# A rewritten preparation, two chunks interleaved ahead of attention, and operands loaded by halves in a fused macaron-block kernel

## The chip, the cores and the metric

The kernel runs on one core of one Trainium2 chip, as one launch. The metric is device time in microseconds (us) of that core; a kernel's time is the median of its runs.

## The reference

```
x = x + 0.5 * ffn(layernorm(x))            # pass A, x is (4, 1024, 128)
x = x + attn(layernorm(x))                 # 16 heads of 8, rotary, ALiBi, softmax over all 1024 keys
x = x + 0.5 * ffn(layernorm(x))            # pass C

def ffn(x):
    shared = relu2(x @ up_w.T) @ down_w.T                 # 512 hidden columns
    scores = sigmoid(x @ gate.T)                          # 8 experts, best group of 2, top 2, normalised
    lat    = x @ fc1_w.T
    routed = sum_e coef_e * (relu2(lat @ w1[e].T) @ w2[e].T)
    return shared + routed @ fc2_w.T

def attn(x):
    q, k, v = heads(x @ qkv_w.T); q, k = rotary(q), rotary(k)
    s = q @ k.T * 8**-0.5 + 8 * slope_h * min(key - query, 0)
    return (softmax(s) @ v) @ proj_w.T + proj_b
```

## The kernel before

The 4096 tokens are 8 chunks of 512 (two halves of each of 4 batches). The program has a preparation block (lines 200 to 370), then one fused block of five engine streams (from line 521), then two blocks that run only when a bound on the scores fails; in the profiled execution only the test of that bound is made.

The preparation loads all weights, turns them on TensorE, folds fc1 with w1 and w2 with fc2, and splits them in a high and a low part (`w_hi`, `w_lo`), since most products are made of three passes (`times_weights`, L709). VectorE collects the weights in `w_all`, ScalarE copies the high part, VectorE subtracts. All its loads are issued by SyncE, the first two x chunks, the rotary table and the row of positions last. The fused block begins when every engine has left the preparation.

In the fused block each chunk is a job of pass A (`("A", c)`: layer norm, router, FFN, residual, second norm, rotary q and k, v) and, after its attention, a job of pass C (`("C", c)`: projection, norm, router, FFN, residual, store). Attention runs over 256 "quads": 32 groups (chunk, four heads) of 8 key tiles. A quad is four score matmuls of 512 columns into the four banks `scores` (L729), one ScalarE exponential of 128x2048 (`weight`, L977), on half of the quads a VectorE multiplication by `ediag` (L1334), and four matmuls with v into `acc` (`weigh`, L748). The four score banks are a single set, so the next quad's scores wait for the exponential.

The order is written out: `PLAN` gives each job's operations a step, every engine walks over the same steps and does at each step what the plan and `+1` rules say (`rectify = hidden + 1`, and so on), and waits for semaphores. Quad n is at step `HEAD_STEPS + n`. Before the first quad (`HEAD_STEPS` = 58) stand jobs A0 and A1, nearly all of A2 (32 of 40 matmul operations) and a third of A3 (13 of 40); after the last quad (from step 314) stand 10 operations of C5, 31 of the 32 of C6 and all of C7. An engine's stream is strictly in order. In a job the relu of a hidden tile is ScalarE's (L945), the square or the product of relu and expert coefficient is GpSimd's (L1003) behind VectorE's `scale` (L1231), the router is VectorE's (`route1` to `route5`, L1142 to L1216), `res` the end of the FFN (L1237). `relu` is a ring of four tiles that every job shares, as are `xn`, `xn_t` and the banks `bank_h`, `bank_c`, `bank_o`; only in the "wide" jobs A0, A1 and C7 are the score banks used as second banks.

The rotary q and k are split in parts and stored to DRAM (L640), and loaded again, transposed by address, as the operands `q_op`, `k_full`, `k_plain`: per batch 4 groups x 12 loads of both halves at once (`load_parts`, L2076) and 8 loads of the shift row (L675). All are SyncE's. The rows of these operands that don't come from DRAM are filled by GpSimd at the first 12 steps (`fill_rows`). The load of the x chunk of A3 (L634) follows the residual of A1 in the plan. `ediag` is made in the preparation.

## Time and profile before

| what | us |
|---|---|
| median of 3 runs | 897.0 (896.61 to 901.86) |
| profiled execution, its own time | 895.53 |
| span of that execution, first to last instruction | 893.7 |
| preparation, to the first instruction of the fused block | 22.35 |
| first exponential of attention | 163.5 |
| end of the last exponential | 824.1 |
| last residual | 874.8 to 875.5 |

The page gives for the span of 893.7 us: TensorE busy 755.8 us (85%), VectorE 468.2 (52%), ScalarE 577.5 (65%), GpSimd 239.1 (27%). Times in the rows are microseconds from the start of the span unless they say ns. The 1.8 us between the span and the execution's own time lie outside the instructions.

### The profile page before, as it was taken

How to read it: one execution, taken by the hardware profiler on the slowest of the kernel's cores; microseconds unless marked ns; L12 is line 12 of the kernel's file. 1: busy time of each engine (PE TensorE's matmuls, PEld its weight loads, DVE VectorE, ACT ScalarE, POOL GpSimd, SP SyncE). 2: the span in 40 equal slices, each digit the busy share in tenths (PEclk: the TensorE clock that was granted, in tenths of full speed). 3: DMA queues.
4: the chain of work that ended last, by engine and by line, in shares of the span. 5: the costliest groups of instructions: out<-in, count | busy, mean ns of one | idle time of the engine just before them, and what ended most of it. 6: DMA issues, size and time to landing. Idle time of an engine off the chain costs nothing. (4 is left out here: it accounts for less than half of the span.)

```text
span 893.7 us, 14584 instructions
## 1 busy us (share of the span) xinstructions
PE 755.8 (85%) x5517; PEld 372.6 (42%) x5517; DVE 468.2 (52%) x1171; ACT 577.5 (65%) x439; POOL 239.1 (27%) x207
## 2 busy tenths in 40 slices
PE   3567781889899999989999899989999999989881
PEld 2456560334344334434434344334444344434561
DVE  4877771744634755462563553653554635354770
ACT  2121110578778877777887788977888788888220
POOL 1855440401301331221231122221122211213350
PEclk9997996799999999899999999999999999999996
DMA  6002057111122451120233210034421001010100
GB/s 217 1 23 71 25 136 171 38 39 28 40 77 68 100 149 51 28 64 19 70 87 99 66 47 4 16 91 100 104 62 53 5 5 54 4 52 4 55 12 20
DMA packets 42071, 52.64 MB, mean 59 GB/s; under 512 B 9528, under 2 KB 27392, under 8 KB 41856
## 3 DMA queue, kind: packets, MB, share of 16 engines
q1 hardware_dynamic: 41984, 51.53, 21.7%
q8 instruction: 49, 0.80, 0.4%
q14 instruction: 38, 0.31, 0.1%
HBM read 31.85 MB, written 19.40 MB: 57 GB/s over the span
## 5 line engine op out<-in xcount | busy, mean ns | idle before, releaser
L977 ACT ACTIVATE weights<-f_scores 128x2048 f32<-128x2048 f32 x256 | 481.0, 1879 | 126.8 <-PE f_scores L729 121.4
L748 PE MATMUL f_acc<-weights,v_res 128*9 128x512 f32 x2048 | 270.1, 599 | 12.7 <-DVE weights L1334 11.5
L1334 DVE TENSOR_TENSOR weights<-weights,ediag 128x512 f32<-128x512 f32 x128 | 92.8, 726 | 113.2 <-ACT weights L977 112.9
L824 PE MATMUL f_bank_o<-w_out,f_hid 128*128 128x128 f32 x1024 | 146.2, 288 | 2.3 <-POOL f_hid L1003 1.8
L1003 POOL TENSOR_TENSOR f_hid<-f_hid,f_relu 128x512 f32<-128x512 f32 x64 | 86.6, 1357 | 228.1 <-DVE f_hid L1231 226.8
L824 PEld LDWEIGHTS f_bank_o<-w_out,f_hid 128*128 128x128 f32 x1024 | 125.6, 194 | 51.9 <-issue 40.0
L1003 POOL TENSOR_TENSOR f_hid<-f_relu 128x512 f32<-128x512 f32 x64 | 68.0, 1068 | 251.9 <-ACT f_relu L945 248.5
L945 ACT ACTIVATE f_relu<-f_bank_h 128x512 f32<-128x512 f32 x116 | 69.0, 595 | 83.3 <-PE f_bank_h L709 80.8
L729 PE MATMUL f_scores<-q_op,k_plain 29*128 29x512 f32 (+3 forms) x768 | 86.8, 441 | 19.8 <-ACT weights L977 15.8
L729 PEld LDWEIGHTS f_scores<-q_op,k_plain 29*128 29x128 f32 x768 | 37.5, 183 | 137.0 <-ACT weights L977 112.8
L709 PE MATMUL f_bank_h<-f_xn_t,w_hi 128*128 128x512 f32 x232 | 86.4, 454 | 9.5 <-ACT f_relu L945 6.8
L1231 DVE TENSOR_TENSOR f_hid<-f_relu,f_bank_c 128x512 f32<-128x512 f32 x58 | 39.7, 685 | 95.7 <-ACT f_relu L945 88.1
L729 PE MATMUL f_scores<-q_op,k_full 29*128 29x512 f32 (+3 forms) x640 | 62.1, 375 | 7.6 <-ACT weights L977 5.6
L748 PEld LDWEIGHTS f_acc<-weights,v_res 128*9 128x9 f32 x2048 | 31.3, 88 | 72.6 <-issue 60.2
L709 PEld LDWEIGHTS f_bank_h<-f_xn_t,w_hi 128*128 128x128 f32 x232 | 36.5, 195 | 57.8 <-issue 41.9
L729 PEld LDWEIGHTS f_scores<-q_op,k_full 29*128 29x128 f32 x640 | 31.6, 185 | 51.2 <-ACT weights L977 50.2
L709 PE MATMUL f_bank_h<-f_xn_t,w_lo 128*128 128x512 f32 x116 | 47.2, 407 | 0.0
L810 PE MATMUL f_bank_c<-f_coef_t,spread_rows 128*128 128x512 f32 x58 | 24.8, 427 | 25.9 <-DVE f_hid L1231 25.8
L1327 DVE COPY f_o_out<-f_acc 128x512 f32<-128x512 f32 x32 | 22.0, 688 | 28.1 <-PE f_acc L748 28.1
L1019 POOL TENSOR_TENSOR f_squares<-f_roped 128x512 bf16<-128x512 f32 x16 | 19.5, 1218 | 56.6 <-DVE f_roped L1272 49.9
L991 POOL TENSOR_TENSOR f_rstd<-f_veps,f_minus_half 128x4 f32<-128x4 f32 x24 | 24.3, 1011 | 36.8 <-DVE f_veps L1096 36.8
L709 PEld LDWEIGHTS f_bank_h<-f_xn_t,w_lo 128*128 128x128 f32 x116 | 22.6, 195 | 5.6
(165 smaller groups left out, 703.6 us busy)
## 6 DMA issues: line engine op xcount, KB each, us to landing
q_parts<-f_parts SPq DMA_DIRECT2D x24, 256.0 KB, 3.0
k_parts<-f_parts SPq DMA_DIRECT2D x24, 256.0 KB, 3.0
q_op<-q_parts SPq DMA_DIRECT2D x64, 96.0 KB
k_full<-k_parts SPq DMA_DIRECT2D x64, 96.0 KB
k_plain<-k_parts SPq DMA_DIRECT2D x64, 96.0 KB
o_scratch<-f_o_out SPq DMA_DIRECT2D x128, 18.0 KB
x_ln<-in_L_attn_x_dram SPq DMA_DIRECT2D x8, 256.0 KB, 2.9
rope<-const_rope SPq DMA_DIRECT2D x1, 2048.0 KB, 9.5
```

Of the source, the lines that this page charges most:

```text
L709: last = nc.tensor.matmul(out, w[:, col:col + P], x_t[:, part, :], start=(i == 0), stop=(i == 2))
L729: last = nc.tensor.matmul(scores[:, j, lo:hi], k_op[rows, g, kt * P:(kt + 1) * P], q_op[rows, g, CHUNK * half + lo:CHUNK * half + hi], sta ...
L748: last = nc.tensor.matmul(acc[BLOCK * j:BLOCK * j + VW, :], v_res[:, c // HALVES, kt, col:col + VW], weights[:, n % 2, j, :], start=(kt == ...
L810: nc.tensor.matmul(spread_bank(job, m), spread_rows[:, m * P:(m + 1) * P], coef_t[:, :], start=True, stop=True).then_inc(spread, 1)
L824: last = nc.tensor.matmul(bank_o[:, t * P:(t + 1) * P], hid[:, m, t * P:(t + 1) * P], w_out[:, m, :], start=(m == 0 and t == 0), stop=(m = ...
L945: nc.scalar.activation(relu[:, at % RELUS, :], hidden_bank(job, m), ACT.Relu).then_inc(relu_ready, 1)
L977: nc.scalar.activation(weights[:, n % 2, :, :], scores[:, :, :], ACT.Exp).then_inc(exps_done, 1)
L991: nc.gpsimd.tensor_tensor(rstd[:, which, :], veps[:, which, :], minus_half[:, :], ALU.pow).then_inc(rstd_ready[which], 1)
L1003: nc.gpsimd.tensor_tensor(hid[:, m, :], other, relu[:, at % RELUS, :], ALU.mult).then_inc(hid_ready, 1)
L1231: v.tensor_tensor(hid[:, ST + m, :], relu[:, at % RELUS, :], spread_bank(job, m), ALU.mult).then_inc(scaled_ready, 1)
L1327: v.tensor_copy(o_out[:, :], acc[:, :]).then_inc(acc_read, 1)
L1334: v.tensor_tensor(at, at, ediag[:, GH * g:GH * (g + 1), :], ALU.mult).then_inc(diag_done, 1)
```

## The change

1. Preparation. The weight loads are split over two issuing engines: SyncE issues the fold weights, the two x chunks, the tables, `diag` and `rope`; ScalarE issues up, qkv, gate, the slopes, down, proj, a new constant `turn` and the positions. `w_all` is gone: ScalarE writes the high parts straight from the banks and VectorE subtracts from the banks. The rotated columns come from a matmul with `turn`. The norm of chunk 0, up to both parts of its turned tile, is made here too, its square root on GpSimd. `sdiag` is gone; GpSimd's memset of `v_res` covers only the columns of ones, and GpSimd fills `k_plain` of two groups.
2. Jobs A0 and A1 (`HEAD_JOBS`). They are interleaved over 222 finer steps, each operation with a step of its own (`own=...`, kept in `job.at`). A1 has its own banks (`acc` for `bank_o`, `scores[:, 1]` and `[:, 3]` for the gate and the turn) and tiles (`twin_xn`, `twin_xn_t`), and relu tiles of both are not in the shared ring. In these two jobs the squares are ScalarE's and only once per tile (`relu` squared, then VectorE multiplies by the coefficient), and ScalarE also copies the coefficients and the high parts of q and k.
3. ScalarE also fills `q_op` and `k_full` (`FILLS`, 8 instructions of 128x1024) and makes `ediag` (`DIAGONALS`, 16 exponentials of 128x128 with a scale) during these steps.
4. Operands of batch 0. They are loaded per half and group: 8 times 12 loads of 48 KB, and per group 2 loads of the shift row. Group 0's first half follows the store of A0; the rest follows the shift, or the quads. Group 0's shift rows are issued by ScalarE. Scores wait for `first_loaded`, `late_plain` and `late_loaded`.
5. The plan. The first quad is at step 222 with A0 and A1 complete and 12 of the 40 matmul operations of A2 ahead of it; 9 instead of 3 of the 256 attention steps are without an operation of a job. After the last quad (from step 478) stand 14 operations of C4, 31 of C5 and all 32 of both C6 and C7. The x load of A3 is at step 130.

```diff
-HEAD_STEPS = 58
+HEAD_JOBS = 2
+HEAD_STEPS = 222
+FILLS = (2, 69, 151, 118, 6, 109, 51, 59)
+DIAGONALS = (136, 133, 156, 137, 141, 142, 144, 123, 132, 125, 146, 122, 139, 147, 131, 128)
 PLAN = (
+    ("A", 0, dict(front=(0, 0, 0), norm=(-9, -9, -9, 0), route=(8, 13, 18, 23, 28), coef=35,
+        hidden=(3, 7, 12, 21, 25, 30, 41, 49), spread=(39, 48, 55, 62),
+        outs=(15, 15, 27, 27, 32, 32, 44, 44, 52, 52, 56, 56, 64, 64, 70, 70), residual=77,
+        norm2=(80, 93, 124), qk=(140, 143, 150, 157), value=(152, 152), norms=(168, 183),
...
+    ("A", 1, dict(front=(0, 0, 0), norm=(1, 16, 19, 37), route=(43, 53, 60, 67, 72), coef=90,
+        hidden=(61, 68, 73, 78, 83, 91, 99, 107), spread=(98, 106, 114, 119),
+        outs=(75, 75, 86, 86, 94, 94, 102, 102, 111, 111, 115, 115, 120, 120, 126, 126), residual=130,
+        norm2=(138, 158, 163), qk=(174, 176, 179, 182), value=(187, 187), norms=(191, 199),
...
+            def square(job, m):
+
+                act.wait_ge(relu_ready, HT * job.index + m + 1)
+                tile = relu_tile(job, m)
+                nc.scalar.activation(tile, tile, ACT.Square).then_inc(squared, 1)
...
+            def fill_rows(i):
+
+                which, g = divmod(i, HG)
+                op, factor, add = ((q_op, row_sel[:, 6:7], q_add1), (k_full, row_sel[:, 3:4], k_add1))[which]
+                nc.scalar.activation(op[:, g, :], pos, ACT.Identity, bias=add[:, g:g + 1], scale=factor).then_inc(rows_filled, 1)
...
+            def first_operands(step):
+                if step == FIRST_JOB[0].at["store"][1] + 1:
+                    load_half(0, 0, first_loaded[0], first_loaded[0])
+                if step == FIRST_JOB[1].at["fill"] + 1:
+                    sp.wait_ge(shift_ready, 1)
+                    load_half(1, 0, late_plain, late_loaded)
+                    load_half(0, 1, first_loaded[1], first_loaded[1])
+                    load_shift_rows(sp, 0, 1, first_loaded[1])
+                for g in range(1, HG):
+                    if g >= 2 and step == HEAD_STEPS + KT * (g - 1) + 2:
+                        sp.wait_ge(shift_ready, 1)
+                        load_half(0, g, first_loaded[g], first_loaded[g])
+                        load_shift_rows(sp, 0, g, first_loaded[g])
+                    if step == HEAD_STEPS + KT * (g - 1) + 4:
+                        sp.wait_ge(late_plain, 16 * GH * g)
+                        sp.wait_ge(late_loaded, 16 * (PART_LOADS - GH) * g)
+                        load_half(1, g, late_plain, late_loaded)
...
+                if half == 0 and batch == 0 and kt == 0:
+                    pe.wait_ge(first_loaded[g], 16 * (PART_LOADS + HALVES))
+                elif half == 0 and batch == 0 and kt == TILES:
+                    pe.wait_ge(late_plain, 16 * GH * (g + 1))
+                elif half == 1 and batch == 0 and kt == 0:
+                    pe.wait_ge(late_loaded, 16 * (PART_LOADS - GH) * (g + 1))
```

## Rows read from the trace of the kernel before

**Rows 1.** Windows: us, busy (instructions) per engine, granted TensorE clock, DMA share, GB/s.
```profile
core 0: us, PE busy (x) PEld busy (x) DVE busy (x) ACT busy (x) POOL busy (x), PEclk, DMA share, GB/s
0.00:22.35 22.35, 8.20 (x28) 5.62 (x28) 9.61 (x27) 6.17 (x7) 4.13 (x6) 1.00 0.64 217
22.35:60.28 37.93, 23.63 (x121) 19.74 (x122) 28.07 (x72) 6.42 (x12) 25.83 (x24) 0.96 0.00 1
60.28:96.11 35.83, 28.49 (x142) 22.68 (x141) 27.31 (x77) 7.41 (x13) 17.68 (x15) 0.81 0.20 59
96.11:122.20 26.09, 17.39 (x84) 11.13 (x83) 22.30 (x61) 6.09 (x11) 15.31 (x14) 1.00 0.21 61
122.20:137.00 14.80, 12.03 (x78) 9.33 (x78) 11.56 (x41) 2.98 (x5) 5.11 (x5) 1.00 0.69 165
137.00:157.90 20.90, 0.49 (x5) 0.25 (x3) 0.00 (x0) 1.08 (x2) 0.00 (x0) 0.61 0.75 163
...
163.50:824.10 660.60, 618.78 (x4784) 268.73 (x4784) 328.69 (x795) 534.46 (x367) 145.05 (x123) 0.99 0.21 55
824.10:876.00 51.90, 43.03 (x273) 33.05 (x269) 35.10 (x86) 12.25 (x22) 22.48 (x20) 1.00 0.10 29
876.00:893.70 17.70, 0.00 (x0) 0.00 (x0) 0.00 (x0) 0.00 (x0) 0.00 (x0) 0.58 0.09 25
```

**Rows 2.** Waits between 124 and 163 us.
```profile
DVE f_stats L1077 <- DMA x_ln<-in_L_attn_x_dram: 21.3, 1, 21.3
```

**Rows 3.** Timeline of SyncE's issues: start, us, instruction.
```profile
125.01 0.33 SPq L2076 DMA_DIRECT2D q_op<-q_parts  x1
...
145.39 4.46 SPq L675 DMA_DIRECT2D q_op<-f_shift  x8
...
150.39 0.50 SPq L634 DMA_DIRECT2D x_ln<-in_L_attn_x_dram  x1
```

**Rows 4.** Timeline of ScalarE, first quads; its idle time before in brackets.
```profile
163.55 1.88 ACT L977 ACTIVATE weights<-f_scores 128x2048 f32<-128x2048 f32 x1 [1.42 <-PE f_scores L729]
166.33 1.88 ACT L977 ACTIVATE weights<-f_scores 128x2048 f32<-128x2048 f32 x1 [0.91 <-PE f_scores L729]
169.83 1.88 ACT L977 ACTIVATE weights<-f_scores 128x2048 f32<-128x2048 f32 x1 [1.62 <-PE f_scores L729]
172.32 1.88 ACT L977 ACTIVATE weights<-f_scores 128x2048 f32<-128x2048 f32 x1 [0.61 <-PE f_scores L729]
```

**Rows 5.** Timeline: second weight set turned, `sdiag`, last split, first gate.
```profile
8.88 0.48 PE L306 MATMUL prep<-ident,raw_up 128*128 128x128 f32 x1 [2.33 <-DMA raw_proj<-in_L_attn_proj_w_dram]
...
15.64 2.28 DVE L349 TENSOR_TENSOR sdiag<-diag,slope 128x2048 f32<-128x2048 f32 x1
...
21.39 0.68 DVE L369 TENSOR_TENSOR w_lo<-w_all,w_hi 128x512 fp32r<-128x512 f32 x1
...
33.66 0.21 PE L775 MATMUL f_bank_c<-w_gate,f_xn_t 128*128 128x16 f32 x1
```

**Rows 6.** Timeline of VectorE: a norm's centring, a router's first and 16th instruction, statistics.
```profile
67.90 1.10 DVE L1100 TENSOR_SCALAR f_xn<-f_res,f_mean,f_rstd 128x128 f32<-128x128 f32 x4
...
87.59 0.19 DVE L1142 TENSOR_TENSOR f_en<-f_en 128x32 f32<-128x32 f32 x1 [2.66 <-ACT f_en L937]
...
92.21 0.42 DVE L1195 TENSOR_REDUCE f_rank<-f_above 128x32 f32<-128x256 f32 x1
...
98.82 0.86 DVE L1077 BATCH_NORM_STATS2 f_stats<-f_res 128x6 f32<-128x128 f32 x4
```

**Rows 7.** Groups by line, whole page: VectorE's scale, ScalarE's relu, GpSimd's squares.
```profile
L1003 POOL TENSOR_TENSOR f_hid<-f_hid,f_relu 128x512 f32<-128x512 f32 x64 | 86.6, 1357 | 228.1 <-DVE f_hid L1231 226.8
L945 ACT ACTIVATE f_relu<-f_bank_h 128x512 f32<-128x512 f32 x116 | 69.0, 595 | 83.3 <-PE f_bank_h L709 80.8
L1231 DVE TENSOR_TENSOR f_hid<-f_relu,f_bank_c 128x512 f32<-128x512 f32 x58 | 39.7, 685 | 95.7 <-ACT f_relu L945 88.1
```

**Rows 8.** Timeline of ScalarE in the preparation.
```profile
0.72 1.28 ACT L285 ACT_TABLE_LOAD   x1 [0.72 <-PEq L2357]
...
13.11 0.28 ACT L285 ACTIVATE proj_t<-prep 128x128 f32<-128x128 f32 x1
13.32 1.27 ACT L285 ACTIVATE w_hi<-w_all 128x1280 fp32r<-128x1280 f32 x1
```

**Rows 9.** Timeline of VectorE: the residuals of C5, C6 and C7.
```profile
833.24 0.63 DVE L1237 SCALAR_TENSOR_TENSOR f_res<-f_bank_o,f_x 128x512 f32<-128x512 f32 x1
...
857.00 0.68 DVE L1237 SCALAR_TENSOR_TENSOR f_res<-f_bank_o,f_x 128x512 f32<-128x512 f32 x1
874.78 0.69 DVE L1237 SCALAR_TENSOR_TENSOR f_res<-f_bank_o,f_x 128x512 f32<-128x512 f32 x1 [4.45 <-PE f_bank_o L824]
```

**Rows 10.** DMA issues: median us from issue to landing of an x chunk.
```profile
x_ln<-in_L_attn_x_dram SPq DMA_DIRECT2D x8, 256.0 KB, 2.9
```

## The prediction before the change was run

> **What bounds the kernel now.** I read the windows first, cut where the stages change. The span of 893.7 us falls in four pieces: up to the first exponential at 163.5, attention from 163.5 to 824.1 (660.6), the last jobs from 824.1 to 876.0 (51.9), and 17.7 in which no engine does any work of the job and the test of the bound and the exit run [rows 1]. The page's averages (TensorE 85%) hide that these pieces have different limits.
>
> Attention goes by a cadence. The timeline shows an exponential every 2.49 us once the stage is running: 1.88 of the exponential itself and 0.61 in which ScalarE waits for the next scores, since the score banks are one set [rows 4]. 256 times 2.49 is 637 us; the stage takes 660.6, so 23 us are stalls. Job work of TensorE fits between the exponentials, and about one operation of a job per quad is what the plan gives it.
>
> The piece ahead of attention is the loose one. From 22.35 to 122.2 TensorE is busy 69.5 of 99.9 us, VectorE 77.7 (28.07 + 27.31 + 22.30), ScalarE only 19.9; at 122 both chunks of batch 0 are done [rows 1]. Then come 41 us more. From 137.0 to 157.9 VectorE does nothing and TensorE 0.49 us, while the DMA engines are 75% busy at 163 GB/s [rows 1]. The waits name the cause: VectorE stood 21.3 us for an x chunk [rows 2]. SyncE's timeline says why: 48 operand loads from 125.0 and 8 shift loads from 145.4 stand ahead of the x load of A3, issued at 150.4 [rows 3], which lands 7.5 us later where the median of such loads is 2.9 [rows 10]. The scores of quad 0 stand behind this on TensorE, since a product of A2 waits for VectorE. So the stage carries A2 and a part of A3, but at a poor price, and 4.6 MB of operands pass before the first quad.
>
> **The change, part by part.**
>
> Preparation. Before, the last split ends at 22.07 and the first gate starts at 33.66, because the loop's first norm, with GpSimd filling rows beside it, comes after the block [rows 5]. Before, the second weight set is not turned until 8.88, VectorE waits till then, and `sdiag` costs it 2.28 [rows 5]. VectorE's new chain: slopes 2 us from about 6, the two fold copies 1, statistics and moments 2 [0.86 of it as in rows 6], two subtractions 1.3, centring 1.1, the small and rotated ones 0.7, the last weight split 0.7, the low part 0.7: its end is near 16 to 17. ScalarE's copies (0.6 per 512 columns by rows 7) end there too. I take 17.5 for the first gate, 33.66 before: bounds 15.5 (all loads early) and 20 (the loads issued on two engines wait for each other; the first 22 us move 217 GB/s on average already [rows 1]).
>
> The Trainium skill (DMA: Bandwidth & Descriptors, section Issuing engines are not separate DMA queues) says that initiating on two engines saves only sequencer time. The rate in rows 1 agrees that the engines are already loaded; by that rule alone this split is worth nothing, and by my chain the first gate is set by VectorE either way.
>
> Jobs A0 and A1 in the loop. VectorE: per job of pass A fifteen instructions of 512 columns (low parts 2, scale 4, residual, rotary products 4, sums 2, largest norms 2) at 0.685 [rows 7] is 10.3; two norms at some 3.0 (0.86 + 1.0 of moments + 1.10 [rows 6]); a router some 6.5 (from 87.59 to 92.63 for its first 16 instructions with one of them stretched [rows 6], and seven of 0.2 more). A0 has one norm and one low part less: 19.1. A1 with the bound: 23.8. Together 43 us. TensorE: the last window has 43.0 us for 73 job operations, 0.59 each [rows 1]; A0 and A1 have 79 in the loop and some three of A2 stand before the shift: 82 x 0.59 = 48. ScalarE: 16 relus and 16 squares at 0.595 [rows 7] are 19; 12 other copies of 512 columns 7; eight fills of 1024 columns, between 0.60 and the 1.27 of 1280 columns [rows 8], 1.05 each: 8.4; sixteen exponentials of 128 columns at 0.28 [rows 8]: 4.5; together 39. GpSimd falls to the low parts, the squares of q and k and the roots, some 15 us.
>
> So three engines have 39 to 48 us. Before, VectorE was busy 78% of 22.35 to 122.2; 43/0.78 is 55. TensorE was busy 80% (28.49 of 35.83) in its densest stretch there, at a granted clock of 0.81 [rows 1]; 48/0.8 is 60. I take 58 us from the first gate to the shift. The lower bound is 50 (48 of TensorE with almost no gap). The upper is 70: 52/0.75, if the half clock returns as in that stretch. A chain can't hide more than this: one chunk alone needs about 36 us of dependent steps from norm to shift, and two are interleaved.
>
> To the first exponential: two shift issues at 0.56 (4.46/8 [rows 3]), landing 2.9 [rows 10], score matmuls 1: 5 us. First exponential at 17.5 + 58 + 5 = 80.5, before 163.5: 83 us earlier. What goes with it is the 21.3 us stall, the operand queue, 11.6 from the norm and three loads of x, and A2's and A3's work, which is not saved but moved.
>
> Operands by halves. Only group 0's first half is on the path, and A0's store comes long before the shift. SyncE has 96 part issues at 0.41 (48 in the 20.4 us of rows 3) and 6 shift issues at 0.56 (group 0's two are ScalarE's): 43 us in all. Behind the shift stand group 0's second half (4.9), then group 1's first half (4.9) and its shift rows (1.1): landed 14 us after the shift. Its `late_plain` part lands after 4.5 and is needed at quad 4, 5 + 10 after the shift; group 1 is needed at quad 8, 5 + 20. Groups 2 and 3 have six steps (15 us) each for 6 us of issue. Behind them on SyncE stand the parts of A2, due at step 248, and the o stores, four per group. Expected cost 0; bounds -2 and +10 (one group late on its DMA: 12 loads of 48 KB are 3.5 us at 163 GB/s).
>
> Attention. The plan's job operations per step are as many as before in all: 3 empty steps before, 9 after. A2 now runs in quads 0 to 30, where before it ended. Early quads before lost 7 us against 2.49 in the first 32. The first three exponentials were 2.78 and 3.50 apart [rows 4]. I leave 660.6, with bounds -4 and +12.
>
> After the last quad. Before: 73 job operations in 51.9 us. After: 14 + 31 + 32 + 32 = 109. By TensorE's 0.59 each that is 36 x 0.59 = 21 more. By jobs, one more whole job: C6 took 23.8 and C7 17.8 us from the residual before it [rows 9], so 18 to 24, plus four operations of C4. By steps, 45 instead of 29 to the last residual. I take +22, bounds +16 and +27. This is the moved work, paid once.
>
> Sum of the span: 80.5 + 660.6 + (51.9 + 22) + 17.7 = 832.7; the profiled execution's own time is 1.8 above its span and the median 1.5 above that: 836.0, that is 61 below 897.0 (83 - 22). No change can be told from 1% either way.
>
> **The rivals.**
>
> R1, the two chunks don't interleave. Streams are in order, ScalarE now holds relu, square, coefficient copy, high parts and fills, and a late step of one chunk holds the other. For it: squares on ScalarE make each relu tile two dependent ScalarE steps where before ScalarE was 20% busy and GpSimd took them. Against: 39 us of ScalarE in 58. If the two run as badly as before, the shift is 100 us after the first gate (22.35 to 122.2), first exponential at 122: 836 + 42 = 878. Half of that, 857, is as likely.
>
> R2, ScalarE must reload tables. The trace has a single ACT_TABLE_LOAD of 1.28 us with Relu, Copy and Exp [rows 8]; Square and Identity are in no row. If they belong to another set, the plan changes between them and Exp 8 times in the head: 8 x 1.28 = 10 us on ScalarE, at most 10 on the path, 846. The Trainium skill (ScalarE: Activation LUTs, section Table sets: the hidden batching unit) puts relu, copy and identity in every set and doesn't name square; its section What ACT_TABLE_LOAD costs has 2.66 us per switch with the drain, by which it would be 21.
>
> R3, the operand halves starve the first groups. If each of groups 1 to 3 comes 7 us late, 20 us: 856. For it: twice the issues, in one queue with the o stores. Against: the sums above.
>
> R4, slower than before: attention runs at the lower clock. With the lean head TensorE might enter attention at 1.2 GHz and stay. At 166.33 to 169.83, when the clock was half granted, a quad took 3.50 instead of 2.49 [rows 4]. The price is 1.0 us a quad, and it decides from 61 of the 256 quads on; with all of them the time would be 1090, with 100 of them 936. Against: attention has 0.99 granted with TensorE busy 94% [rows 1], and recovered by the fourth quad after a 21 us pause.
>
> R5, the change does not shorten the head as the SyncE queue is only moved: excluded but for a part, since the first score needs 12 + 2 loads instead of 56.
>
> **How the numbers follow.** The forecast has 0.77, R1 0.11, R2 0.04, R3 0.05, R4 0.02, and no gain for any other reason 0.01. The forecast's own bounds, taken together and not all at once (head -8 and +12, preparation 2, attention -4 and +12, last jobs -6 and +5), give 822 to 852. To keep no more than 2 in 10 outside I widen to 819 and to 858, which takes in R2, R3 and the better half of R1. Faster by over 1%: all but R4 and the rest, 0.96; same 0.02; slower 0.02.
>
> **What the profile after would show.** First gate at 17 to 18 us with both parts of `xn_t` made in the preparation; first exponential near 80; VectorE and TensorE busy over 75% between, ScalarE 65%, GpSimd little; no wait on x of 20 us; one ACT_TABLE_LOAD; quads 4, 8, 16 and 24 without a wait for a DMA; 660 us from first to last exponential; about 74 us from there to the last residual. The prediction is wrong if the head stage is above 70 us or attention moves by over 12.

## The result and the profile after

The changed kernel takes 845.87 us, median of 5 runs (844.31 to 854.09), where the kernel before took 897.0: ratio 0.9425, 95% interval 0.9391 to 0.9459. Measured twice more, beside the kernel before on the same chip each time, it gave 852.25 (ratio 0.9498, 0.945 to 0.9546) and 853.05 (0.9483, 0.9455 to 0.9512). Over all runs it lies between 844.3 and 855.5, the kernel before between 894.2 and 903.2. 836.0 was forecast, with 819 to 858.

The profiled execution took 854.09 us, 852.2 of it the span. Its windows, cut where the stages change (columns as in [rows 1]):

```profile
0.00:18.86 18.86, 6.88 (x36) 5.25 (x36) 9.79 (x35) 5.67 (x11) 4.46 (x9) 0.96 0.81 260
18.86:79.00 60.14, 52.62 (x286) 42.84 (x287) 44.99 (x145) 40.14 (x72) 18.56 (x19) 0.84 0.24 72
79.00:87.00 8.00, 7.97 (x44) 7.30 (x42) 3.75 (x23) 1.30 (x3) 2.11 (x2) 0.59 0.44 132
87.00:755.50 668.50, 622.62 (x4764) 270.04 (x4764) 335.42 (x814) 535.77 (x370) 150.06 (x125) 0.98 0.23 59
755.50:834.50 79.00, 65.16 (x396) 50.70 (x392) 55.71 (x138) 18.59 (x34) 33.97 (x30) 0.98 0.12 32
834.50:852.20 17.70, 0.17 (x1) 0.07 (x1) 0.17 (x2) 0.00 (x0) 0.00 (x0) 0.56 0.09 25
```

The stages add up to 87.0 + 668.5 + 79.0 + 17.7. Against [rows 1] the head is 76.5 us shorter, the last jobs are 27.1 longer, the exit is the same, and attention took 7.9 more in this execution. Between the preparation and 79 us TensorE is busy 87% and VectorE 75%, where before they had 70% and 78% over a stretch of 100 us.

The start of the loop, from the timelines of VectorE, GpSimd and TensorE, answers to [rows 5]:

```profile
17.14 0.69 DVE L414 TENSOR_TENSOR xn_t<-prep,xn_t 128x512 fp32r<-128x512 f32 x1 [0.30 <-ACT xn_t L305]
...
18.90 0.52 POOL L1273 MEMSET f_coef_t<- 128x512 f32 x1
...
19.52 0.35 PE L933 MATMUL f_bank_c<-w_gate,xn_t 128*128 128x16 f32 x1 [2.62 <-POOL f_coef_t L1273]
```

The operand of the gate is ready at 17.83. All engines then enter the loop at 18.9, and TensorE waits for one more thing: GpSimd's clearing of `coef_t`, the first work in its stream there. The gate is 14.1 us earlier than in [rows 5].

The end of the head, from ScalarE's and TensorE's timelines:

```profile
76.76 0.60 ACT L1120 ACTIVATE f_relu<-f_bank_h 128x512 f32<-128x512 f32 x1 [1.74 <-PE f_bank_h L860]
76.77 1.36 ACTq L752 DMA_DIRECT2D q_op<-f_shift  x2
...
87.02 1.88 ACT L1192 ACTIVATE weights<-f_scores 128x2048 f32<-128x2048 f32 x1
...
89.52 1.88 ACT L1192 ACTIVATE weights<-f_scores 128x2048 f32<-128x2048 f32 x1
```

```profile
78.86 1.91 PE L991 MATMUL f_bank_o<-w_out,f_hid 128*128 128x128 f32 x8
80.42 0.36 PE L933 MATMUL f_bank_c<-w_gate,xn_t 128*128 128x16 f32 x1
...
82.12 3.66 PE L991 MATMUL f_bank_o<-w_out,f_hid 128*128 128x128 f32 x16
85.54 0.71 PE L860 MATMUL f_bank_h<-xn_t,w_hi 128*128 128x512 f32 x2
86.09 0.39 PE L860 MATMUL f_bank_h<-xn_t,w_lo 128*128 128x512 f32 x1
86.41 0.33 PE L886 MATMUL f_scores<-q_op,k_plain 29*128 29x128 f32 x4
```

The shift is written at 75.2. The issue of its rows begins 1.6 us later, since in ScalarE's stream it stands behind a relu of A2, which waits for TensorE; it ends at 78.1. The first scores start only at 86.41 and have no wait in brackets. TensorE is working through A2's outputs and gate until then, most of it at the lower clock of 1.2 GHz: eight `f_bank_o` matmuls take 1.91 us here, where eight take 1.16 at 89.39. At 85.54 the clock is back: two hidden matmuls take 0.71 instead of 1.22 at 77.41.

The wait of 21.3 us for an x chunk [rows 2] is in no line of the waits after. The residuals of C4, C5 and C7 answer to [rows 9] (C6's is at 814.62):

```profile
765.52 0.69 DVE L1428 SCALAR_TENSOR_TENSOR f_res<-f_bank_o,f_x 128x512 f32<-128x512 f32 x1 [1.05 <-PE f_bank_o L991]
791.37 0.68 DVE L1428 SCALAR_TENSOR_TENSOR f_res<-f_bank_o,f_x 128x512 f32<-128x512 f32 x1
...
833.77 0.69 DVE L1428 SCALAR_TENSOR_TENSOR f_res<-f_bank_o,f_x 128x512 f32<-128x512 f32 x1 [4.44 <-PE f_bank_o L991]
```

One correction to what stands above: the x load issued at 150.39 in the kernel before [rows 3] is that of chunk A4, which its plan puts behind A2's residual, and not A3's, which had been issued at 97.25. Nothing in the sum hangs on the name, but the second experiment does.

### The profile page after: what moved, and what is told of

Its sections match the earlier page's. It is cut to its first block and busy times, and to the rows that moved or that the text cites. A ratio compares the mean times of both kernels' runs of the same rounds, so it can differ in the third digit from the quotient of the medians.

```text
span 852.2 us, 14656 instructions
## 1 busy us (share of the span) xinstructions
PE 755.4 (89%) x5521; PEld 376.2 (44%) x5521; DVE 449.8 (53%) x1155; ACT 601.5 (71%) x488; POOL 209.2 (25%) x184
## 5 line engine op out<-in xcount | busy, mean ns | idle before, releaser
L1532 DVE TENSOR_TENSOR weights<-weights,ediag 128x512 f32<-128x512 f32 x128 | 95.3, 746 | 134.9 <-ACT weights L1192 134.5
L1230 POOL TENSOR_TENSOR f_hid<-f_hid,f_relu 128x512 f32<-128x512 f32 x56 | 77.1, 1380 | 205.9 <-DVE f_hid L1422 205.7
L1230 POOL TENSOR_TENSOR f_hid<-f_relu 128x512 f32<-128x512 f32 x56 | 60.9, 1090 | 232.0 <-ACT f_relu L1120 231.9
L1120 ACT ACTIVATE f_relu<-f_bank_h 128x512 f32<-128x512 f32 x110 | 65.4, 594 | 45.6 <-PE f_bank_h L860 41.4
L860 PE MATMUL f_bank_h<-xn_t,w_hi 128*128 128x512 f32 x224 | 83.4, 454 | 8.0 <-ACT f_relu L1120 6.0
L860 PEld LDWEIGHTS f_bank_h<-xn_t,w_hi 128*128 128x128 f32 x224 | 35.0, 195 | 52.0 <-issue 42.9
L860 PE MATMUL f_bank_h<-xn_t,w_lo 128*128 128x512 f32 x112 | 45.2, 404 | 0.0
L1218 POOL TENSOR_TENSOR rstd<-veps,minus_half 128x4 f32<-128x4 f32 x23 | 23.5, 1021 | 71.4 <-DVE veps L449 71.4
L972 PE MATMUL f_bank_c<-f_coef_t,spread_rows 128*128 128x512 f32 x58 | 24.2, 417 | 2.5 <-DVE f_hid L1422 2.4
L860 PEld LDWEIGHTS f_bank_h<-xn_t,w_lo 128*128 128x128 f32 x112 | 21.7, 194 | 5.4
```

The source lines that it names most:

```text
L860: last = nc.tensor.matmul(out, w[:, col:col + P], x_t[:, part, :], start=(i == 0), stop=(i == 2))
L972: nc.tensor.matmul(spread_bank(job, m), spread_rows[:, m * P:(m + 1) * P], coef_t[:, :], start=True, stop=True).then_inc(spread, 1)
L1120: nc.scalar.activation(relu_tile(job, m), hidden_bank(job, m), ACT.Relu).then_inc(relu_ready, 1)
L1218: nc.gpsimd.tensor_tensor(rstd[:, which, :], veps[:, which, :], minus_half[:, :], ALU.pow).then_inc(rstd_ready[which], 1)
L1230: nc.gpsimd.tensor_tensor(hid[:, m, :], other, relu_tile(job, m), ALU.mult).then_inc(hid_ready, 1)
L1532: v.tensor_tensor(at, at, ediag[:, GH * g:GH * (g + 1), :], ALU.mult).then_inc(diag_done, 1)
```

## The experiments

Times of stages are from each kernel's profiled execution: the start of the first exponential of attention, attention from there to the end of the last one, and from there to the start of the last residual. "Ratio" is to the kernel before on the same chip, with its 95% interval. Below the first two rows, each group of four rows was measured side by side on one chip and shares its runs of the kernel before. "Low clock" is the part of the attention stage that TensorE spent at 1.2 GHz, an estimate: the granted clock of windows of 0.5 us, added up.

| kernel | median us | ratio | first exp | attention | low clock | last jobs |
|---|---|---|---|---|---|---|
| before | 897.0 | 1 | 163.5 | 660.6 | 15.6 | 50.7 |
| changed, first profile | 845.87 | 0.9425 (0.9391 to 0.9459) | 87.0 | 668.5 | 27.3 | 78.3 |
| changed, second | 852.25 | 0.9498 (0.945 to 0.9546) | 85.5 | 663.7 | 17.1 | 76.5 |
| operands whole | 849.17 | 0.9457 (0.9412 to 0.9502) | 88.7 | 661.8 | 13.7 | 76.5 |
| before, operand loads later | 878.47 | 0.9771 (0.9724 to 0.9818) | 142.3 | 665.9 | 30.6 | 50.5 |
| A2 later | 848.21 | 0.945 (0.9404 to 0.9497) | 83.5 | 666.0 | 16.4 | 78.0 |
| two more wide jobs | 848.85 | 0.9459 (0.9399 to 0.9518) | 85.6 | 657.2 | 3.4 | 76.2 |
| A0 and A1 in series | 874.42 | 0.9728 (0.9696 to 0.976) | 109.8 | 660.0 | 10.2 | 76.6 |
| added matmuls | 842.65 | 0.9361 (0.9332 to 0.9391) | 83.0 | 663.4 | 17.1 | 77.9 |
| squares on GpSimd | 854.72 | 0.9519 (0.9469 to 0.957) | 98.2 | 660.0 | 10.2 | 76.6 |
| changed, third | 853.05 | 0.9483 (0.9455 to 0.9512) | 88.1 | 668.6 | 27.3 | 77.9 |
| added matmuls, again | 840.91 | 0.938 (0.9346 to 0.9414) | 83.2 | 660.5 | 10.2 | 76.5 |
| + last squares on ScalarE | 838.11 | 0.9322 (0.9291 to 0.9353) | 83.3 | 663.8 | 17.1 | 70.5 |
| + wide | 836.69 | 0.9312 (0.9285 to 0.9339) | 82.8 | 660.8 | 10.2 | 68.9 |

**The changed kernel unaltered.** 

> The changed kernel with nothing altered, beside which the other kernels of this call are read. Expected: 845 to 848 us, first exponential of the attention at 87.0 us, attention 668 us from there, last jobs after it 79 us.

All three stages came out shorter than in the first profile: 85.5 instead of 87.0, 663.7 instead of 668.5, 76.5 instead of 78.3. The profiled run is the shortest of the four (846.25), and the median is 4 to 7 us above what was expected.

The table says where the difference in attention comes from. In all variants of the changed kernel but "operands whole" and "A2 later" this stage is the same, or nearly so. There its length goes with the low clock: 3.4 us of it with 657.2, 10.2 with 660.0 to 660.8, 17.1 with 663.4 to 663.8, 27.3 with 668.5 and 668.6. That is about half a microsecond for each at the lower clock. Differences in attention below are read against that column.

**The queue alone, in the kernel before.**

```
         made = FIRST_JOB[HALVES * batch + 1].store[1] + 1
+        if batch == 0 and g >= 1:
+            made = FIRST_JOB[2].residual + 1
```

> The kernel before, with one thing moved: the loads of groups 1 to 3 of batch 0 are issued behind chunk 2's residual, so that the load of x for chunk 4 stands behind 12 loads of operands and not 48 in SyncE's queue. My theory (the 21.3 us in which VectorE waited for that x, at 124 to 145 us, stood on the path to the first score): the stall goes, the first exponential comes near 142 us in place of 163.5, and the total is near 876. The changed kernel would then owe some 20 us of its gain to where its operand loads stand. Rival (another wait takes the place of the stall, since TensorE still has the same jobs ahead of the first score, or groups 1 to 3 now come late): first exponential at 160 us or later, total 890 to 897.

The x load went out at 132.5 and the first exponential came at 142.3, 21.2 us earlier and within 0.3 us of the theory, from SyncE's and ScalarE's timelines:

```profile
132.51 0.51 SPq L636 DMA_DIRECT2D x_ln<-in_L_attn_x_dram  x1
...
142.30 1.88 ACT L979 ACTIVATE weights<-f_scores 128x2048 f32<-128x2048 f32 x1 [1.25 <-PE f_scores L731]
```

The total fell by 2.3% (interval 1.8 to 2.8), 20.5 us. So about 21 of the 76 us of head that the change saves were a place in a queue, to be had with two lines; the rival, another wait in the same place, is refuted. (Attention took 5.3 us more in this profile than in the one of the kernel before, with 15.0 us more of low clock.)

**Operands whole.**

```
-                if step == FIRST_JOB[0].at["store"][1] + 1:
-                    load_half(0, 0, first_loaded[0], first_loaded[0])
+                if step == FIRST_JOB[1].at["store"][1] + 1:
+                    for side in range(2):
+                        sp.wait_ge(parts_stored[side], 16 * TERMS * HALVES)
+                    sp.wait_ge(rows_filled, 3 * HG)
+                    load_parts(sp, env, 0, 0, first_loaded[0])
                 if step == FIRST_JOB[1].at["fill"] + 1:
...
+                    for g in range(1, HG):
+                        load_parts(sp, env, 0, g, first_loaded[g])
+                        load_shift_rows(sp, 0, g, first_loaded[g])
```

> The changed kernel, but with the operands of batch 0 loaded whole, group by group: group 0 once chunk 1's parts are stored, groups 1 to 3 behind the shift. My theory: the load by halves is worth little, since the parts of chunk 1 are stored only some us before the shift is ready, and the first score waits for TensorE's own queue (the outs and gate of chunk 2) anyway. Group 0's loads would be issued from about 78 to 85.4 us and land near 88.5, so the first exponential comes at about 89.5 (2.5 us later) and the total is 2 to 4 us longer, near 849. Rival (the halves carry much of the gain): the first exponential comes 10 us later or more, groups 1 to 3 starve quads 16 to 48, and the total is 860 or more.

TensorE now waits for the operand itself:

```profile
88.09 0.33 PE L865 MATMUL f_scores<-q_op,k_plain 29*128 29x128 f32 x4 [0.85 <-DMA k_plain<-k_parts]
```

The first exponential is 0.6 to 3.2 us later than in the three profiles of the changed kernel, no quad of groups 1 to 3 starves, and the total can't be told from the unaltered kernel measured beside it (849.17 against 852.25, with intervals that overlap). The loads by halves are worth 0.6 to 3.2 us of head, and nothing that the total shows.

**A2 behind the first score.**

```
-    ("A", 2, dict(front=(0, 0, 0), norm=(97, 113, 129, 219), route=(220, 221, 222, 223, 224), coef=225,
-        hidden=(203, 208, 214, 221, 222, 227, 228, 229), spread=(227, 228, 229, 230),
-        outs=(219, 219, 220, 220, 220, 220, 223, 223, 230, 230, 231, 232, 232, 234, 234, 235), residual=236,
+    ("A", 2, dict(front=(0, 0, 0), norm=(97, 113, 129, 222), route=(223, 224, 224, 225, 226), coef=227,
+        hidden=(203, 208, 214, 222, 223, 227, 228, 229), spread=(228, 229, 229, 230),
+        outs=(222, 222, 223, 223, 224, 224, 225, 225, 230, 231, 231, 232, 232, 234, 234, 235), residual=236,
...
```

> The changed kernel, with the first outs, the gate, and the hidden blocks 3 and 4 of chunk 2 moved behind the first score (steps 219 to 221 become 222 to 226). TensorE worked on them from 78.9 to 86.4 us at half clock, while the shift was ready at 75.2 us and the first operands landed near 78. My theory: these 7.5 us stand on the path; the first exponential comes near 81.5 us (5.5 us earlier), a part is given back in the first quads, and the total is 2 to 4 us shorter, near 843. Rival (the first score waits for its operands or for the store of chunk 1's parts, and TensorE only fills that time): first exponential unchanged at 87 us, total unchanged or, with the work now inside the attention, 2 to 5 us longer.

```profile
79.01 0.63 PE L860 MATMUL f_bank_h<-xn_t,w_lo 128*128 128x512 f32 x1
82.50 0.48 PE L886 MATMUL f_scores<-q_op,k_plain 29*128 29x128 f32 x4 [2.85 <-DMA q_op<-f_shift]
```

Both theories hold in part. TensorE's work had been on the path, for 2 to 4.6 us; with it gone the shift rows are next, 6.7 us after the shift. Attention then begins with intervals of 4.38 and 3.21 us in place of 2.5, which take 2.6 us back, and the total shows no difference: work moved behind the first score was not seen to be saved.

**Two more wide jobs.**

```
-WIDE = (("A", 0), ("A", 1), ("C", 7))
+WIDE = (("A", 0), ("A", 1), ("C", 5), ("C", 6), ("C", 7))
...
-                if job is JOBS[-1] and m == 1:
+                if job.wide and not job.head and m == 1:
```

> The changed kernel, with the jobs of chunks 5 and 6 of the last stage given the two hidden banks that only the last job has (three jobs wide in place of one). After the attention 79.0 us are left, in steps of 25.9, 23.2 and 19.2 us from residual to residual, and the last one is the widest. My theory: in the two narrow jobs TensorE waits for one bank to be emptied by the activation; wide, each comes nearer to 19 to 21 us, and the total is 3 to 6 us shorter, near 841. Rival (the tail runs at the pace of GpSimd's squares or of TensorE itself): 0 to 1 us.

The last jobs took 76.2. That has to be compared at the same clock. Where the clock stayed at 1.00 in this stage (five profiles, the second of the changed kernel among them) the single bank gave 76.5 to 76.6. Where it fell to 0.50 for some 3 us it gave 77.9 to 78.3 (four profiles, the first among them). Here it fell too, near 773 us, so the wide banks are worth 1.7 to 2.1 us: less than the theory's 3 to 6, more than the rival's 0 to 1. The short profiled time (839.45) is an attention of 657.2 with only 3.4 us of low clock, in code that was not touched; the other runs go up to 855.0, so the total shows nothing of this size.

**A0 and A1 in series.**

```
+LATER = 190
+HEAD_STEPS = 222 + LATER
...
+PLAN = (PLAN[0],) + tuple((kind, chunk, later(plan)) for kind, chunk, plan in PLAN[1:])
...
+        twin_xn_t = xn_t[:, :, :]
```

> The changed kernel, but with chunks 0 and 1 one after the other: every step of chunk 1 and of all later jobs stands 190 steps later in the order, and the waits that belong to the interleaving are changed with it; operands by halves, preparation and banks are kept. My theory (interleaving lets each chunk's chain of small steps run under the other's TensorE work): the two chunks took 56 us together from gate to shift, while the chain of one alone took about 45 us for chunk 0 (from its gate to its stored parts), so the first exponential comes at 115 to 120 us and the total is some 30 us longer, near 876. Rival (the gain is from the early start of preparation and from the queue, and TensorE is the bound of the head in either order): first exponential at 87 to 92 us, total at most 5 us longer.

A1 also shares the tile `xn_t` with A0 here. The windows of the head, from the first gate, cut at A0's residual, A1's residual, the shift and the first exponential:

```profile
19.80:39.40 19.60, 18.86 (x104) 16.47 (x104) 7.93 (x28) 15.38 (x24) 2.08 (x2) 1.00 0.01 2
39.40:80.20 40.80, 27.15 (x140) 22.55 (x141) 24.11 (x84) 21.00 (x42) 7.58 (x7) 0.79 0.22 66
80.20:99.40 19.20, 10.62 (x40) 7.06 (x38) 12.36 (x32) 3.65 (x6) 7.11 (x7) 0.79 0.28 83
99.40:109.80 10.40, 9.74 (x46) 8.80 (x46) 4.71 (x29) 1.87 (x4) 3.14 (x3) 0.56 0.39 125
```

From gate to shift 79.6 us instead of 55.7. In the first window TensorE is busy 96% even with one chunk, since the FFN feeds it; in the two behind it only 63%, in the norm, the rotary products and the bound. The interleaving is worth 22 to 24 us in the head and, by the ratios to the kernel before, 2.3 to 3.0% of the time (21 to 27 us). I had expected 30: one chunk's FFN runs almost without gaps alone.

**Squares of A0 and A1 back on GpSimd.**

```
-                    if job.head and job.at["square"][m] == step:
-                        square(job, m)
...
+            def square_head(job, m):
+                pool.wait_ge(relu_ready, HT * job.index + m + 1)
+                tile = relu_tile(job, m)
+                nc.gpsimd.tensor_tensor(tile, tile, tile, ALU.mult).then_inc(squared, 1)
```

> The changed kernel, with the squares of the hidden activations of chunks 0 and 1 on GpSimd, as in all later jobs, in place of ScalarE (16 squares). This undoes one part of the change. My theory: on GpSimd one takes about 1.05 us against 0.6 on ScalarE and stands later in each chain, and VectorE's work beside it is stretched; the first exponential comes 3 to 6 us later, near 91, the total near 850. Rival (ScalarE, 45 us busy of 60, was the tighter engine and is relieved): first exponential 1 to 3 us earlier.

GpSimd's timeline:

```profile
24.36 1.04 POOL L1233 TENSOR_TENSOR f_hid<-f_hid 128x512 f32<-128x512 f32 x1 [0.48 <-ACT f_hid L1120]
25.64 2.04 POOL L1233 TENSOR_TENSOR f_hid<-f_hid 128x512 f32<-128x512 f32 x2 [0.24 <-ACT f_hid L1120]
...
51.71 3.04 POOL L1233 TENSOR_TENSOR f_relu<-f_relu 128x512 f32<-128x512 f32 x3
```

A square is 1.04 us here, as expected, and 0.24 to 0.5 us pass from the relu to its start, where ScalarE goes on at once. The shift comes 10 us later (85.9), the first exponential 10 to 12.7 later: two to three times what I expected. (The 45 us that the rival gives ScalarE are VectorE's figure; ScalarE was busy 40.1.) The total shows less: the ratio of 0.9519 is 2 to 8 us above the three of the changed kernel, and its interval overlaps two of theirs. Of the head, 10 us are the squares' place; the prediction counted their ScalarE time but gave them no gain of their own.

**46 added matmuls.**

```
             for step in range(STEPS):
+                if step == 126:
+                    pe.wait_ge(scaled_ready, RT * HEAD_JOBS)
+                if 126 <= step < 218 and step % 2 == 0:
+                    nc.tensor.matmul(bank_c[:, :], w_hi[:, 0:P], spread_rows[:, :], start=True, stop=True)
```

> The changed kernel with 46 additional matmuls of 128x128 by 128x512 whose result nobody reads, one at every second step from 126 to 216 (about 57 to 79 us), to keep TensorE busy where it pauses between the pieces of chunk 1. From 60 to 87 us the granted clock was 0.50 to 0.78. My theory: the pauses bring the clock down, the slower clock costs the outs and gates in that stretch, and with the filling the clock stays near 1.0, so the first exponential comes 5 to 7 us earlier, near 81, and the total is 4 to 7 us shorter. Rival (the path there is VectorE's and ScalarE's chain, and additional matmuls only stand ahead of the wanted ones): first exponential unchanged or 1 to 5 us later.

Windows of the changed kernel, and under it the same with the added matmuls (second measurement):

```profile
60.00:66.00 6.00, 4.02 (x12) 2.68 (x13) 4.42 (x8) 1.23 (x2) 2.58 (x3) 0.64 0.42 131
66.00:72.00 6.00, 4.78 (x21) 3.16 (x19) 5.04 (x7) 1.75 (x3) 3.63 (x4) 0.78 0.56 167
72.00:78.00 6.00, 4.48 (x8) 2.25 (x9) 3.12 (x12) 1.19 (x2) 3.10 (x4) 0.50 0.65 195
78.00:84.00 6.00, 6.00 (x28) 5.80 (x27) 1.30 (x10) 0.82 (x2) 1.51 (x2) 0.50 0.51 161
```

```profile
60.00:66.00 6.00, 6.00 (x31) 4.46 (x31) 5.50 (x9) 1.85 (x4) 3.66 (x4) 1.00 0.42 131
66.00:72.00 6.00, 6.00 (x31) 4.30 (x30) 4.72 (x7) 1.67 (x3) 3.66 (x4) 1.00 0.45 141
72.00:78.00 6.00, 5.76 (x23) 3.60 (x21) 4.92 (x13) 1.28 (x3) 3.69 (x5) 1.00 0.37 102
78.00:84.00 6.00, 5.80 (x48) 4.93 (x46) 2.98 (x18) 2.12 (x4) 3.00 (x4) 1.00 0.85 255
```

The clock stays at 2.4 GHz where it had been at 1.2 for much of the time, and from 78 to 84 TensorE does 48 matmuls in place of 28. How long it is low there differs between executions of the changed kernel: its second profile had more of the full clock, and its first exponential at 85.5.

```profile
78.00:84.00 6.00, 5.73 (x36) 5.44 (x36) 1.22 (x8) 1.04 (x3) 2.08 (x2) 0.72 0.75 228
```

The shift is at most 1.7 us later (written at 75.8 and 76.9, against 75.2 to 76.3), and the gain lies behind it. From A2's first hidden matmul to the last of its outputs ahead of the scores the changed kernel takes 12.8 us in its third profile (clock 0.50 from 78 to 84) and 10.0 in its second (0.72); with the added matmuls it is 7.7 (1.00), though these stand in between. The issue of the shift rows begins at most 0.6 us after the shift in place of 1.3 to 1.6. First exponential at 83.0, 2.5 to 5 us earlier.

> The kernel with 46 additional unread matmuls again, beside the changed kernel on the same chip. If what it gained (first exponential at 83.0 us, granted clock 1.00 from 57 to 88 us) is its doing, its median lies 3 to 7 us below that of the changed kernel here too. Rival (the gain of the first look was the scatter of the changed kernel's runs): the two intervals overlap.

Beside the unaltered kernel on the same chip the intervals don't overlap: 0.938 (0.9346 to 0.9414) against 0.9483 (0.9455 to 0.9512), 9 us by the ratios. That is more than the head gives. Of the 14.0 us between the two profiled executions 4.9 lie in the head, 8.1 in attention and 1.4 in the last jobs, less 0.4 at the exit; see the last section.

> The changed kernel again, unaltered, in the same call as the three kernels below and with more rounds, since its runs so far lie between 844.3 and 855.5 us. Expected: median 846 to 852 us, first exponential between 85.5 and 87.0 us, and among its runs a shorter time where the mean granted clock is higher.

The median is 1 us above the expected band and the first exponential at 88.1. The two shortest of its six runs (849.1, 849.2) have mean clocks of 0.962 and 0.963, the longest (855.3) 0.955, though one of 852.9 has 0.964; with the added matmuls all are between 0.972 and 0.987.

**The last squares on ScalarE too.**

```
+TAIL = 12
...
                     if job.at["rectify"][m] == step:
                         rectify(job, m)
+                        if job.tail and m >= ST:
+                            square(job, m)
...
+                elif job.tail:
+                    dve.wait_ge(squared, HT * HEAD_JOBS + RT * (job.index - TAIL) + m + 1)
```

> The kernel with the 46 additional matmuls, and in the jobs of chunks 4 to 7 of the last stage the squares of the gated hidden blocks are taken by ScalarE, in place, ahead of the multiplication by the spread coefficients, as in chunks 0 and 1, in place of by GpSimd behind it. Putting the squares of the first two chunks back on GpSimd cost 11 us of head for two jobs. Theory 1 (in the last jobs too, GpSimd's 1.28 us at the end of each spread-scale-square chain, and its delay of the reciprocal roots, stand on the path): the 76.5 us from the end of the last exponential of the attention to the last residual become 70 to 73, total 3 to 6 us below the kernel with the additional matmuls alone. Theory 2 (the last jobs run at the pace of TensorE and of VectorE's routing, and GpSimd's squares hide): 0 to 1 us.

ScalarE's timeline shows relu and square of a gated tile back to back. In VectorE's the product that ends the chain stands behind a norm's centring:

```profile
771.99 0.60 ACT L1136 ACTIVATE f_relu<-f_bank_h 128x512 f32<-128x512 f32 x1 [0.45 <-PE f_bank_h L868]
772.62 0.63 ACT L1142 ACTIVATE f_relu<-f_relu 128x512 f32<-128x512 f32 x1
```

```profile
773.15 1.11 DVE L1305 TENSOR_SCALAR xn<-f_x,mean,rstd 128x128 f32<-128x128 f32 x4 [0.19 <-POOL rstd L1236]
774.18 0.68 DVE L1442 TENSOR_TENSOR f_hid<-f_relu,f_bank_c 128x512 f32<-128x512 f32 x1
```

The last jobs take 70.5 us in place of 76.5, both at a clock of 1.00: theory 1 and its number. The median falls by 2.8 us only, 0.9322 against 0.938 with intervals that overlap; the profiled attention was 3.3 longer, with 6.9 us more of low clock.

> The same kernel with the jobs of chunks 5 and 6 of the last stage wide too (two hidden banks, as the last job has). Alone, the wide banks took 0.4 us off the last jobs. If GpSimd's squares had hidden what the wide banks bring, the two together take 2 us or more off the kernel with the ScalarE squares alone; if VectorE's routing sets these jobs, at most 0.5 us.

With wide banks 68.9, 1.6 less, again at a clock of 1.00. The 0.4 us that the expectation gives the wide banks alone was read across different clocks; at the same clock it was 1.7 to 2.1. So they bring about the same with and without the squares on ScalarE, and GpSimd's squares had hidden nothing of it. The median is 1.4 lower, which the runs can't confirm. The windows of the last jobs with the added matmuls alone, and with all three edits:

```profile
743.70:820.20 76.50, 63.69 (x396) 49.16 (x392) 54.88 (x136) 18.60 (x33) 34.21 (x30) 1.00 0.12 34
```

```profile
743.60:812.50 68.90, 59.86 (x400) 49.14 (x392) 50.63 (x137) 27.39 (x48) 14.34 (x14) 1.00 0.13 37
```

16 squares have gone from GpSimd (34.2 to 14.3) to ScalarE (18.6 to 27.4), and TensorE's share rises from 83 to 87%. This version, 836.69 us, is the fastest, 6.9% below the kernel before and 1.8% below the changed one measured beside it.

## Why the prediction was right, and where it was off

The direction, the mechanism and the range held: a head shorter by 76.5 us, given back in part by last jobs longer by 27. The forecast was low by 10 us against the first median and by 16 to 17 against the later ones; those two, 852.3 and 853.1, lie just beyond the 822 to 852 of the forecast's own bounds, in the part that was added to the range. By its steps, for the first profiled execution (852.2 against 832.7, 19.5 too little):

- **Preparation, 17.5 (15.5 to 20): 19.5.** VectorE's chain ended at 17.83 though its centring took 2.75 instead of 1.1. What the sum left out is the entry into the loop, 1.1 us, and the clearing of `coef_t`, 0.52, which the diff moves to GpSimd as its first work there. The split over two issuing engines did nothing for the start: TensorE's first transposition is at 7.3, where it was at 5.3. That agrees with the rule of the Trainium skill cited in the prediction (DMA: Bandwidth & Descriptors, section Issuing engines are not separate DMA queues), by which a second issuing engine saves only sequencer time; the new order of loads is in it too.
- **Gate to shift, 58 (50 to 70): 55.7.** Right, with VectorE busy 45.0 and ScalarE 40.1 in that window, where 43 and 39 were counted. Before, it was 88.5 (from 33.66 [rows 5] to 122.2 [rows 1]). Undone one at a time, the interleaving is worth 24 of the 33 us between, and the squares on ScalarE 10; the two may overlap. R1 priced a failure of the interleaving at 42 or 21; measured, it is 22 to 24. It took the stage before as 100 us from gate to shift, which counts from the start of the loop and not from the gate.
- **Shift to first exponential, 5: 11.8.** This step failed. It took issue, landing and scores, and no TensorE work, although the plan has A2's gate, eight of its outputs and a hidden block at steps 219 to 221. They ran at the lower clock until about 85.5. Nor is 5 reached without them: 7.7 with A2 moved away (the issue begins 1.6 after the shift, behind a relu that waits for TensorE, and the scores wait for the rows until 3.8 after its end, where 2.9 was taken), 6.3 to 7.2 with the added matmuls.
- **Attention, 660.6 (-4 to +12): 668.5.** The seven other profiles with this stage unaltered have 657.2 to 668.6, so the term was right for some executions and 8 too low for others; the first profile lies at the long end. All are within the bound. The kernel before had 15.6 us of low clock in its 660.6, this execution 27.3: by half a microsecond each that is 5 to 6 of the 7.9, an estimate. The prediction carried the stage over as one execution had shown it, with that execution's share of low clock.
- **Operands by halves, 0 (-2 to +10): nothing lost.** R3 is refuted: quads 4, 8, 16 and 24 start at most 2.63 us after the one before, where 2.49 is the cadence. Of the scores of batch 0 only quad 4's waited for an operand, 0.56 us; the first quad of batch 1 waited 0.95.
- **Last jobs, +22 (16 to 27): +27.1.** The mechanism is right and the size just above its upper bound. From [rows 9]: the additional whole job took 25.9 instead of 18 to 24, C7 19.2 instead of 17.8, the remainder of the job before 10.0 instead of 9.2, and C6 0.5 less. Some 1.4 to 1.8 of it is a fall of the clock in C5; in the second profile, without it, the additional job took 24.2. TensorE's busy time grew by 22.1, as 36 operations at 0.59 have it; the other 5.0 are additional idle time. A job there also has its chain of router, spread, product and GpSimd's square, and the last two experiments, on this chain and on the hidden banks, took 7.6 us off.
- **Exit, 17.7: 17.7.**
- **R2** is refuted: the trace has one table load, at 5.80 us and 1.28 long, with Relu, Copy, Exp, Square and Identity on ScalarE; no run shows what a second one would cost. **R4** did not occur at its price, but its cause did: the lower clock cost the head 2.5 to 5 us, and attention has 3.4 to 27.3 us of it.
- **A reading.** The load that stood behind the 48 operand loads was A4's, not A3's (above); the wait and its price are the same.

## What to carry to other kernels

Before a big rewrite of a stage, look at what stands in the queue ahead of the load that its longest wait is for: here two lines gave 21 of 76 us. When work is moved out of a stage, price it where it lands, by a whole job there and not by the mean of an engine; and an engine that falls idle there (ScalarE behind the last exponential) should take work from the chain, 6 us here. Where a stage ends on a chain of VectorE, ScalarE and DMA steps, look at the clock at which TensorE comes out of it. And before two profiles of a stage are compared, compare their granted clocks: here 3 us at the lower clock hid what the wide banks bring.

## What the runs showed of the hardware

TensorE work that nobody reads made the kernel faster. With 46 matmuls of 128x512 in the gaps of a stretch (60 to 78 us) where TensorE was busy 67 to 80% at a granted clock of 0.50 to 0.78, the clock was 1.00. Without them the clock of the same stretch differs between executions, 0.71 to 0.87 in two profiles (the second, and the one with two more wide jobs) and 0.50 to 0.78 in the first and third.

The scatter of the changed kernel, 11 us between runs of the same program, is in the profiled executions the same thing. The first and third profiles have six falls of the clock in attention, at the same distances from the first exponential (12, 172, 397, 527, 568 and 585 us), 27.3 us of low clock together, and an attention of 668.5 and 668.6. The other profiles have fewer, some of them at the same places, and a shorter stage (the table). Windows of attention in the third profile and, in the second fence, in the kernel with the added matmuls, measured beside it:

```profile
250.00:300.00 50.00, 45.47 (x327) 18.02 (x325) 28.09 (x67) 38.86 (x28) 12.69 (x11) 0.93 0.30 75
```

```profile
250.00:300.00 50.00, 44.98 (x353) 17.83 (x346) 34.19 (x76) 41.27 (x30) 12.53 (x11) 1.00 0.29 77
```

In windows of 3 us the first shows the clock fall to 1.2 GHz for some 6 us, behind three windows in which TensorE was busy 69 to 77%:

```profile
252.00:255.00 3.00, 2.31 (x16) 0.79 (x12) 0.70 (x2) 2.37 (x2) 0.00 (x0) 1.00 0.73 190
255.00:258.00 3.00, 2.27 (x24) 0.99 (x28) 1.45 (x3) 2.08 (x2) 1.57 (x1) 1.00 0.73 169
258.00:261.00 3.00, 2.06 (x25) 0.83 (x26) 2.07 (x4) 2.26 (x3) 0.00 (x0) 0.95 0.67 141
261.00:264.00 3.00, 3.00 (x16) 1.69 (x16) 1.13 (x5) 1.91 (x2) 0.00 (x0) 0.50 0.04 12
264.00:267.00 3.00, 3.00 (x16) 2.07 (x12) 0.40 (x2) 1.74 (x1) 0.00 (x0) 0.50 0.04 9
```

The two quads there took 4.35 and 3.58 us in place of 2.5. Ahead of this fall the first quad of batch 1 waits for its shift rows:

```profile
255.32 0.33 PE L886 MATMUL f_scores<-q_op,k_plain 29*128 29x128 f32 x4 [1.01 <-DMA q_op<-f_shift]
```

The other kernel passed the same place without that wait, with pauses of 0.67 and 1.01 us for VectorE's products, at 1.00. The wait isn't needed for a fall: with A0 and A1 in series and with the squares on GpSimd the clock fell at the same place, 172 us after the first exponential, without it.

What the added matmuls have to do with attention stays open. With them the four profiles have 10.2 to 17.1 us of low clock there, but the kernels without them have 3.4 to 27.3, so their profiles don't separate the two. In the mean clocks (0.972 to 0.987 against 0.955 to 0.964) about half of the difference is the head itself, which has 0.94 against 0.83 in the two profiles. So the 2.5 to 5 us of head are explained by the added matmuls; the rest of the 9 us is measured, it goes with the clock, and why the clock fell less often there was not settled.
